# Graph network layers on one core: the rows of stage 2 turned by 32x32 blocks on VectorE, with sixteen SBUF-to-SBUF transfers a group

## The chip, the cores and the metric

The kernel runs on one core of a Trainium2 chip. The metric is the time of one execution on the device in microseconds (us), lower is better. The kernel before takes 2451.24 us, the median of three runs (2449.91 to 2452.41).

## What is computed

`x` holds 50000 nodes of 256 channels in float32, `edge_attr` 12500 edges, sorted by `dst`. Cut to what matters:

```
h   = relu(layernorm(x))                       # rows
agg = scatter-add over dst of relu(h[src] + edge_attr)
z   = (h + agg) @ W1 + b1                      # 50000 x 512
r   = relu(batchnorm(z))                       # statistics over all nodes
y   = r @ W2 + b2                              # 50000 x 256
x1  = x + h + relu(graph norms of y)           # statistics over all of y
h1  = relu(layernorm(x1))
out = x1 + relu(h1 @ W + segment_sum((h1 @ M)[src], dst))
```

## The kernel before, in words

Nodes are worked on in 98 groups of 512 (four rows to each of 128 partitions; the last group is smaller). Stage 1 (to about 435 us) makes the layer norm factors and the batch statistics and writes the edge sums to a table in HBM. Stage 2 (about 440 to 1600 us) is where the change is. Stage 3 makes `x1` and `h1 @ W`, stage 4 does the edges of the second layer.

Each engine has its own program, and they meet through counting semaphores. For a group k of stage 2:

- SyncE (SP) issues, in this order in one step: the load of the rows x of group k (line 975), which from group 12 on waits until the write of the same buffer, four groups earlier, has landed (line 974); the write of x + h of group k-3 (line 982), which waits for GpSimd's addition; the write of y of group k-6 (line 989); and a blank write (line 993). Groups 0 to 7 stay in SBUF and are not written.
- GpSimd (POOL) waits until the rows of group k-2 have been turned (line 1011), clears `ar`, gathers the edge sums of group k into it with four indirect transfers (line 1020), and then adds h to x for group k-2 (line 1032).
- ScalarE (ACT) makes h from x (`norm`, line 1052), two groups ahead.
- VectorE (DVE) adds h and the gathered sums into `ar` (`add`, line 1132), two groups ahead.
- TensorE (PE) turns `ar` with eight 128x128 transposes into PSUM (`turn`, line 1252), one group ahead. ACT copies this into `tH` in the rounded format fp32r (`keep_high`, line 1094), and DVE takes the rest of it into `tL` (`keep_low`, line 1143).
- TensorE does 24 matmuls with W1 in four quarters m (`hidden`, line 1268), each quarter followed by six matmuls of the group before with W2 (`output`, line 1284). ACT drains each quarter of `hidden` (line 1067), DVE splits it into a high part (`high`, line 1175) and a low part (`low`, line 1184), ACT drains y (line 1081), and DVE takes its statistics (`stats`, line 1155).

The order on DVE in one step k is: statistics 0 of group k-2, `keep_low` of k+1, statistics 1, `high` and `low` 0 and 1 of k, `add` of k+2, `high` and `low` 2 and 3. On ACT it is: y of k-2, `keep_high` of k+1, then `hidden` 0, two pieces of `norm` of k+2, `hidden` 1, two pieces, `hidden` 2 and 3. `ar` and `tH` and `tL` have two buffers each; `r32` and the PSUM targets of a quarter have one.

`rounds` writes the first rounds of four groups out and runs the rest in a loop on the engine; the number written out is `NPEEL` (one round for TensorE).

Of the kernel before, what the change touches and what calls it, by code (L numbers as in the profile page):

```python
# [12 lines left out]
P = 128  # L13
# [16 lines left out]
CA = CH + 16  # L30

# [112 lines left out]
def gnn_kernel(nc, x, src, dst, edge_attr, W1, b1, bn_gamma, bn_beta, W2, b2, ln_w, ln_b,  # L144
# [13 lines left out]
    with ExitStack() as ctx:  # L158
# [32 lines left out]
        Ws = sb("Ws", [P, KC, CH])  # L191
        Ms = sb("Ms", [P, KC, CH])
# [33 lines left out]
        loaded = sem("loaded")  # L226
# [72 lines left out]
        with ExitStack() as scope, nc.Block() as block:  # L299
# [130 lines left out]
            def _(pool):  # L430
# [78 lines left out]
                pool.wait_ge(loaded, 16 * 2)  # L509
# [5 lines left out]
            def _(act):  # L515
# [75 lines left out]
                act.dma_start(Ws[:], W.rearrange("(k p) n -> p k n", p=P)).then_inc(loaded, 16)  # L591
                act.dma_start(Ms[:], M.rearrange("(k p) n -> p k n", p=P)).then_inc(loaded, 16)
# [298 lines left out]
        def turn_over(pe, target, times):  # L891

            for _ in range(times):
                pe.matmul(target, ident[:], Ws[:].rearrange("p a b -> p (a b)"), start=True, stop=True)  # L894
# [16 lines left out]
        NPEEL = KEPT // NU + 2  # L911
# [3 lines left out]
        def stays(k):  # L915
            return is_int(k) and k < KEPT

# [9 lines left out]
        h2_done = sem("h2_done")  # L927
        t2_made = sem("t2_made")
# [11 lines left out]
        with ExitStack() as scope, nc.Block() as block:  # L940
# [21 lines left out]

            @block.sync
            def _(sp):

                def step(at):
# [36 lines left out]
            def _(pool):  # L1003

                def step(at):
                    if inside(at, NG):
# [4 lines left out]
                        after(pool, t2_made, k - AU + 1)  # L1011
# [26 lines left out]
            def _(act):  # L1038
# [46 lines left out]
                def keep_high(at):  # L1085
                    if not inside(at, NG):
                        return
                    k = at[0]
                    s, _ = ring(at, 2)
                    n = columns(k)  # L1090
                    act.wait_ge(t2_made, k + 1)
                    after(act, z_made, (k - 1) * HC)
                    for c in range(KC):
                        last = act.activation(tH[:, s, c, 0:n], hT_ps[:, c, 0:n], ACT.Copy)
# [28 lines left out]
            def _(dve):  # L1123
# [11 lines left out]
                def keep_low(at):  # L1135
# [6 lines left out]
                    for c in range(KC):  # L1142
                        last = dve.tensor_tensor(tL[:, s, c, 0:n], hT_ps[:, c, 0:n],
                                                 tH[:, s, c, 0:n].bitcast(FP32), ALU.subtract)
                    last.then_inc(tl_kept, 1)

# [40 lines left out]
                def step(at):  # L1187
                    stats(back(at, 2), 0)
                    keep_low(back(at, -1))
# [5 lines left out]
                    add(back(at, -2))  # L1195
                    high(at, 2)
# [39 lines left out]
                add((1, 1, 0, NU))  # L1236
                keep_low((0, 0, 0, NU))
# [3 lines left out]
            def _(pe):  # L1241
                def turn(at):
                    if not inside(at, NG):
# [5 lines left out]
                    after(pe, tl_kept, k)  # L1249
# [63 lines left out]
                rounds(pe, step, WHOLE - 2, NU, 1, NG - WHOLE + 2 + 1)  # L1313
# [26 lines left out]

        xy_in = [sem(f"xy_in{s}") for s in range(RL)]
# [32 lines left out]
        with ExitStack() as scope, nc.Block() as block:  # L1374
# [24 lines left out]
            def _(sp):  # L1399
# [258 lines left out]
            def _(pe):  # L1658
                def step(at):
# [304 lines left out]
```

## Time and profile before

| | |
|---|---|
| median of 3 runs | 2451.24 us |
| span of the profiled execution | 2446.4 us |
| PE busy | 2354.5 us (96%) |
| DVE busy | 2052.5 us (84%) |
| ACT busy | 1713.3 us (70%) |
| POOL busy | 1708.5 us (70%) |
| SP's queue q1 | 182434 packets, 459.36 MB, 51.2% of 16 DMA engines |

The profile gives one execution's span from its first to its last instruction and no other time of it; the median of the runs stands 4.8 us above that span. Busy time counts an instruction from start to end, with time in which it is held up inside. PE is the matmuls, PEld the weight loads beside them. SPq is the issue of a transfer on SP: its duration is the engine's time for the issue, not that of the transfer. The granted clock of TensorE is 1.00 at 2.4 GHz and would be 0.50 at 1.2 GHz; a stretch that mixes the two stands between.

### The profile page before, as it was taken

How to read it: one execution, taken by the hardware profiler on the slowest of the kernel's cores; microseconds unless marked ns; L12 is line 12 of the kernel's file. 1: busy time of each engine (PE TensorE's matmuls, PEld its weight loads, DVE VectorE, ACT ScalarE, POOL GpSimd, SP SyncE). 2: the span in 40 equal slices, each digit the busy share in tenths (PEclk: the TensorE clock that was granted, in tenths of full speed). 3: DMA queues.
4: the chain of work that ended last, by engine and by line, in shares of the span. 5: the costliest groups of instructions: out<-in, count | busy, mean ns of one | idle time of the engine just before them, and what ended most of it. 6: DMA issues, size and time to landing. Idle time of an engine off the chain costs nothing. (4 is left out here: it accounts for less than half of the span.)

```text
span 2446.4 us, 48745 instructions
## 1 busy us (share of the span) xinstructions
PE 2354.5 (96%) x12271; PEld 2013.5 (82%) x12271; DVE 2052.5 (84%) x5707; ACT 1713.3 (70%) x3449; POOL 1708.5 (70%) x1599
## 2 busy tenths in 40 slices
PE   7999998799999999999999999979999999989997
PEld 6888886588888888888888888858989888969996
DVE  8999997598888888888888888967777777749996
ACT  6999997466666666666666666638888888846664
POOL 5777777577767667767766666717777777767774
PEclk8999999899999999999999999999999999999999
DMA  8888995323444444444444344349999999765662
GB/s 257 283 278 275 278 277 170 124 58 127 152 150 158 163 151 147 146 146 166 153 147 145 145 164 154 141 173 405 405 411 413 413 413 413 294 197 162 173 177 88
DMA packets 242978, 531.73 MB, mean 217 GB/s; under 512 B 53856, under 2 KB 141177, under 8 KB 231442
## 3 DMA queue, kind: packets, MB, share of 16 engines
q1 hardware_dynamic: 182434, 459.36, 51.2%
q0 software_dynamic: 59808, 70.24, 10.2%
q8 instruction: 50, 0.82, 0.1%
q14 instruction: 94, 0.77, 0.1%
q10 hardware_dynamic: 592, 0.54, 0.1%
HBM read 340.23 MB, written 286.84 MB: 256 GB/s over the span
## 5 line engine op out<-in xcount | busy, mean ns | idle before, releaser
L1020 POOL DMA_INDIRECT ar<-sum_table,idx x392 | 462.3, 1179 | 177.6 <-issue 96.5
L1067 ACT ACTIVATE r<-pair,bnC,bnA 128x512 f32<-128x512 f32 x392 | 305.9, 781 | 380.2 <-PE pair L1268 377.7
L1471 POOL DMA_INDIRECT x1d_table<-x1r,slot x392 | 383.8, 979 | 139.8 <-issue 123.9
L1175 DVE CAST rH<-r 128x512 fp32r<-128x512 f32 x392 | 391.0, 997 | 97.7 <-ACT r L1067 97.7
L1694 PE MATMUL pair<-Ws,h1T 128*128 128x256 f32 x1568 | 358.7, 382 | 8.9 <-DVE orr L1602 7.4
L1694 PEld LDWEIGHTS pair<-Ws,h1T 128*128 128x128 f32 x1568 | 290.2, 190 | 52.1 <-issue 14.3
L1284 PE MATMUL bank<-rH,W2h 128*128 128x512 f32 (+1 forms) x784 | 305.6, 390 | 1.8 <-ACT yr L1081 1.8
L1284 PE MATMUL bank<-rL,W2h 128*128 128x512 f32 (+1 forms) x784 | 305.7, 390 | 0.0
L1284 PE MATMUL bank<-rH,W2l 128*128 128x512 f32 (+1 forms) x784 | 305.0, 389 | 0.0
L836 PE MATMUL bank<-hr 128*128 128x257 f32 (+1 forms) x1568 | 274.2, 329 | 9.6 <-ACT hr L535 9.6
L1184 DVE TENSOR_TENSOR rL<-r,rH 128x512 fp32r<-128x512 f32 x392 | 271.1, 691 | 13.5
L836 PEld LDWEIGHTS bank<-hr 128*128 128x128 f32 x1568 | 251.3, 192 | 36.6 <-ACT hr L535 10.3
L1268 PE MATMUL pair<-tH,W1h 128*128 128x512 f32 (+1 forms) x784 | 250.7, 401 | 0.0
L1268 PE MATMUL pair<-tH,W1l 128*128 128x512 f32 (+1 forms) x784 | 242.7, 391 | 0.0
L1268 PE MATMUL pair<-tL,W1h 128*128 128x512 f32 (+1 forms) x784 | 241.3, 389 | 0.0
L1602 DVE SCALAR_TENSOR_TENSOR orr<-pair,x1r 128x1024 f32<-128x1024 f32 x98 | 120.0, 1224 | 138.2 <-DMA out<-orr 79.5
L1032 POOL TENSOR_TENSOR xr<-xr,hr 128x1024 f32<-128x1024 f32 x90 | 219.9, 2444 | 7.1 <-ACT hr L1052 4.9
L1013 POOL MEMSET ar<- 128x1024 f32 x98 | 95.3, 973 | 173.0 <-PE pair L1252 158.5
L1529 ACT ACTIVATE h1r<-x1r,n,r 128x256 f32<-128x256 f32 x392 | 202.6, 593 | 0.0
L535 ACT ACTIVATE hr<-xr,nmr,rstd 128x256 f32<-128x256 f32 x392 | 202.3, 586 | 0.2
L1052 ACT ACTIVATE hr<-xr,nmr,rstd 128x256 f32<-128x256 f32 x360 | 195.7, 596 | 0.0
L1284 PEld LDWEIGHTS bank<-rH,W2h 128*128 128x128 f32 x784 | 147.3, 188 | 32.6 <-ACT yr L1081 2.5
(239 smaller groups left out, 5234.1 us busy)
## 6 DMA issues: line engine op xcount, KB each, us to landing
xr<-in_x SPq DMA_DIRECT2D x186, 512.0 KB, 3.9
xy_kept<-xy_table SPq DMA_DIRECT2D x57, 1024.0 KB, 20.7
x_table<-x1r SPq DMA_DIRECT2D x97, 512.0 KB, 19.8
out<-orr SPq DMA_DIRECT2D x97, 512.0 KB
xy_table<-xr SPq DMA_DIRECT2D x89, 512.0 KB, 2.6
xy_table<-yr SPq DMA_DIRECT2D x89, 512.0 KB, 3.3
xyr<-xy_table SPq DMA_DIRECT2D x32, 1024.0 KB, 21.0
sum_table<-e_tot SPq DMA_DIRECT2D x99, 128.0 KB, 4.5
```

The source lines that it names most:

```text
L535: last = act.activation(hr[0:p, h, j, 0:CH], xr[0:p, s, j, :], ACT.Relu, bias=nmr[0:p, bass.ds(k * T + j, 1)], scale=rstd[0:p, bass.ds(k * ...
L836: return pe.matmul(o, a, b, start=False, stop=False, skip_group_check=True)
L1020: pool.indirect_dma_start(ar[0:p, s, j, :], None, sum_table[:, :], bass.IndirectOffsetOnAxis(ap=idx[0:p, s, j:j + 1], axis=0), bounds_chec ...
L1032: pool.tensor_tensor(xbuf(k, s)[0:p, 0:n, :], xbuf(k, s)[0:p, 0:n, :], hr[0:p, h, 0:n, :], ALU.add).then_inc(xh2_done, 1)
L1067: act.activation(r32[:, m, 0:n], z_ps[m][:, 0:n], ACT.Relu, bias=bnC[:, m:m + 1], scale=bnA[:, m:m + 1]).then_inc(r_kept, 1)
L1175: dve.tensor_copy(rH[:, s, m, 0:n], r32[:, m, 0:n]).then_inc(rh_kept, 1)
L1184: dve.tensor_tensor(rL[:, s, m, 0:n], r32[:, m, 0:n], rH[:, s, m, 0:n].bitcast(FP32), ALU.subtract).then_inc(rl_kept, 1)
L1268: last = pe.matmul(z_ps[m][:, 0:n], w[:, c, m * P:(m + 1) * P], t[:, s, c, 0:n], start=i == 0, stop=i == len(parts) - 1)
L1284: last = pe.matmul(y_ps[c][:, 0:n], w[:, m, c * P:(c + 1) * P], t[:, s, m, 0:n], start=m == 0 and i == 0, stop=m == HC - 1 and i == 2)
L1471: pool.indirect_dma_start(x1d_table[:, :], bass.IndirectOffsetOnAxis(ap=slot[0:p, part, s * T + j:s * T + j + 1], axis=0), x1r[0:p, s, j, ...
L1529: last = act.activation(h1r[0:p, f, j, :], x1r[0:p, s, j, :], ACT.Relu, bias=n3[0:p, s, j:j + 1], scale=r3[0:p, s, j:j + 1])
L1694: last = pe.matmul(tile_of(pair[2], j)[0:p, :], h1T[:, s, c, j * p:j * p + p], Ws[:, c, :], start=c == 0, stop=c == KC - 1)
```

## The change

TensorE's transposes stay for the first and the last group only. For groups 1 to 96, VectorE turns `ar` in blocks of 32x32 in one instruction (`turn_blocks`) into one buffer `blocks` (the place of W2s). Then SP exchanges the quarters of partitions with sixteen transfers (`move_blocks`), each from 32 partitions to 32 partitions in two pieces of 512 B, 32 KB in all, into one of two buffers `staged` (the places of the stage 3 weights and of W1s). ACT and DVE read `tH` and `tL` from there and not from PSUM. `keep_high` moves behind quarter 1 on ACT, `keep_low` behind `add` on DVE, with `turn_blocks` of the next group behind it. GpSimd's wait for the turned rows becomes one for `blocks_made`. Stage 2 is written out in full on every engine. The weights W and M of stage 3 are loaded at the start of that stage.

```diff
-        NPEEL = KEPT // NU + 2
+        NPEEL = NG
+        def by_tensor(k):
+            return is_int(k) and k in (0, NG - 1)
+        blocks = W2s[:].rearrange("p a b -> p (a b)")
+        staged = [WM[:].rearrange("p a b c -> p (a b c)"), W1s[:].rearrange("p a b -> p (a b)")]
...
+            def turned_part(k, s, c, n):
+                if by_tensor(k):
+                    return hT_ps[:, c, 0:n]
+                return staged[s][:, c * GC:(c + 1) * GC].rearrange("p (q t n) -> p t q n", q=QUADS, t=T)
...
+                def move_blocks(at):
+                    if not inside(at, NG) or by_tensor(at[0]):
+                        return
+                    k = at[0]
+                    s, _ = ring(at, 2)
+                    sp.wait_ge(blocks_made, k)
+                    if is_int(k) and k == 1:
+                        sp.wait_ge(q_made, 1)
+                    after(sp, tl_kept, k - 1)
+                    for q in range(QUADS):
+                        for b in range(QUADS):
+                            here = blocks[q * SQ:(q + 1) * SQ, :].rearrange("p (c b n) -> p c b n", c=KC, b=QUADS)
+                            there = staged[s][b * SQ:(b + 1) * SQ, :].rearrange("p (c q n) -> p c q n", c=KC, q=QUADS)
+                            sp.dma_start(there[:, :, q, :], here[:, :, b, :]).then_inc(ht_in[s], 16)
...
                     three = back(at, 3)
+                    move_blocks(three)
                     if inside(three, NG) and not stays(three[0]):
...
-                        after(pool, t2_made, k - AU + 1)
+                        if is_int(k) and k == AU:
+                            pool.wait_ge(t2_made, 1)
+                        else:
+                            after(pool, blocks_made, k - AU)
...
-                    act.wait_ge(t2_made, k + 1)
+                    if by_tensor(k):
+                        act.wait_ge(t2_made, 1 if k == 0 else 2)
+                    else:
+                        act.wait_ge(ht_in[s], 16 * QUADS * QUADS * turned_before(at))
...
                     keep_y(back(at, 2))
-                    keep_high(back(at, -1))
                     pieces = norm(back(at, -2))
                     for m in range(HC):
                         hidden(at, m)
                         for piece in (pieces[0:2], pieces[2:4], [], [])[m]:
                             piece()
+                        if m == 1:
+                            keep_high(back(at, -1))
...
+                def turn_blocks(at):
+                    if not inside(at, NG) or by_tensor(at[0]):
+                        return
+                    k = at[0]
+                    s, _ = ring(at, AU)
+                    other, _ = ring(back(at, 1), 2)
+                    dve.wait_ge(h2_done, k + 1)
+                    after(dve, ht_in[other], 16 * QUADS * QUADS * turned_before(back(at, 1)))
+                    dve.transpose(blocks.rearrange("p (b t n) -> p t b n", b=KC * QUADS, t=T),
+                                  ar[:, s, :, :].rearrange("p t (b n) -> p t b n", n=SQ)).then_inc(blocks_made, 1)
...
                     stats(back(at, 2), 0)
-                    keep_low(back(at, -1))
                     stats(back(at, 2), 1)
                     high(at, 0)
                     low(at, 0)
                     high(at, 1)
                     low(at, 1)
                     add(back(at, -2))
+                    keep_low(back(at, -1))
+                    turn_blocks(back(at, -2))
                     high(at, 2)
...
-                    if not inside(at, NG):
+                    if not inside(at, NG) or not by_tensor(at[0]):
                         return
...
-                rounds(pe, step, WHOLE - 2, NU, 1, NG - WHOLE + 2 + 1)
+                rounds(pe, step, WHOLE - 2, NU, NPEEL, NG - WHOLE + 2 + 1)
...
+                sp.dma_start(Ws, W.rearrange("(k p) n -> p k n", p=P)).then_inc(w_loaded, 16)
+                sp.dma_start(Ms, M.rearrange("(k p) n -> p k n", p=P)).then_inc(w_loaded, 16)
...
+                        if is_int(k) and k == 0:
+                            pe.wait_ge(w_loaded, 32)
```

## Rows read from the trace of the kernel before

**Rows 1.** Windows: stretch, busy us (instructions) of each engine, clock, DMA share, GB/s.

```profile
1000.00:1200.00 200.00, 200.00 (x952) 167.04 (x951) 172.69 (x221) 122.99 (x204) 138.70 (x119) 1.00 0.43 151
...
2100.00:2200.00 100.00, 89.17 (x484) 74.56 (x483) 60.47 (x201) 63.22 (x131) 69.84 (x73) 0.97 0.62 218
```

**Rows 2.** Timeline of PE in stage 2: start, length, line, work, count.

```profile
475.10 0.40 PE L1284 MATMUL bank<-rH,W2h 128*128 128x512 f32 x1
...
484.65 1.03 PE L1252 MATMUL pair<-ident,ar 128*128 128x128 f32 x8
485.44 0.71 PE L1268 MATMUL pair<-tH,W1h 128*128 128x512 f32 x2
```

**Rows 3.** Groups of instructions, 700 to 1500 us (68 groups of nodes).

```profile
L1020 POOL DMA_INDIRECT ar<-sum_table,idx x272 | 316.4, 1163 | 125.0 <-issue 68.0 <-POOL idx L1014 56.9
L1175 DVE CAST rH<-r 128x512 fp32r<-128x512 f32 x271 | 267.5, 987 | 64.3 <-ACT r L1067 64.3
...
L1184 DVE TENSOR_TENSOR rL<-r,rH 128x512 fp32r<-128x512 f32 x271 | 187.8, 693 | 9.3
...
L1032 POOL TENSOR_TENSOR xr<-xr,hr 128x1024 f32<-128x1024 f32 x68 | 166.7, 2451 | 1.6
...
L1143 DVE TENSOR_TENSOR tL<-pair,tH 128x512 fp32r<-128x512 f32 x136 | 87.3, 683 | 6.4 <-ACT tH L1094 5.4
...
L1132 DVE TENSOR_TENSOR ar<-ar,hr 128x1024 f32<-128x1024 f32 x68 | 83.4, 1227 | 0.0
...
L1013 POOL MEMSET ar<- 128x1024 f32 x68 | 66.5, 977 | 116.9 <-PE pair L1252 116.7
...
L1014 POOL COPY idx<-ids 128x4 int32 x68 | 12.2, 179 | 0.0
```

**Rows 4.** Waits of SP's queue, 700 to 1500 us: total, times, longest.

```profile
SPq L982 <- POOL xr L1032: 565.6, 67, 10.7
SPq L975 <- DMA xy_table<-xr: 62.9, 68, 1.1
```

**Rows 5.** Timeline of SP's issues, about one step of stage 2.

```profile
1111.20 0.33 SPq L982 DMA_DIRECT2D xy_table<-xr  x1
...
1113.95 0.35 SPq L975 DMA_DIRECT2D xr<-in_x  x1
```

**Rows 6.** Timeline of POOL, ACT and DVE in the same step.

```profile
1108.10 3.21 DVE L1175 CAST rH<-r 128x512 fp32r<-128x512 f32 x1 [0.39 <-ACT r L1067]
1108.61 2.40 POOL L1032 TENSOR_TENSOR xr<-xr,hr 128x1024 f32<-128x1024 f32 x1
...
1111.95 0.42 DVE L1175 CAST rH<-r 128x512 fp32r<-128x512 f32 x1
...
1112.46 1.09 ACT L1094 ACTIVATE tH<-pair 128x512 fp32r<-128x512 f32 x2
...
1113.62 1.27 DVE L1143 TENSOR_TENSOR tL<-pair,tH 128x512 fp32r<-128x512 f32 x2
```

**Rows 7.** Timelines of issues without a wait between them: stage 1, then stage 2.

```profile
1.87 0.41 SPq L391 DMA_DIRECT2D src_rows<-in_src  x1
...
3.92 0.36 SPq L395 DMA_DIRECT2D id_table<-no_rows  x1
...
33.77 0.27 ACTq L589 DMA_DIRECT2D vec_rows<-in_L_gnn_bn_gamma  x1
...
36.28 0.41 ACTq L591 DMA_DIRECT2D Ws<-in_L_gnn_W  x1
...
447.80 0.46 SPq L993 DMA_DIRECT2D x1d_table<-blank  x1
448.30 0.43 SPq L975 DMA_DIRECT2D xy_kept<-in_x  x1
```

**Rows 8.** Transfers: what, queue, count, KB each, median us to landing.

```profile
xy_table<-xr SPq DMA_DIRECT2D x89, 512.0 KB, 2.6
...
id_table<-no_rows SPq DMA_DIRECT2D x1, 196.0 KB, 2.1
```

More of the change, by code:

```diff
@@ L30 @@
 CA = CH + 16
+SQ = 32
+QUADS = P // SQ
 def back(at, lag):
@@ L190, in gnn_kernel @@
         W2l = sb("W2l", [P, HC, CH], FP32R, scope=weights, side="right")
-        Ws = sb("Ws", [P, KC, CH])
-        Ms = sb("Ms", [P, KC, CH])
+        WM = sb("WM", [P, 2, KC, CH])
+        Ws, Ms = WM[:, 0, :, :], WM[:, 1, :, :]
         vec = sb("vec", [P, 24])
@@ L893, in turn_over @@
             for _ in range(times):
-                pe.matmul(target, ident[:], Ws[:].rearrange("p a b -> p (a b)"), start=True, stop=True)
+                pe.matmul(target, ident[:], W1s[:, 0, :], start=True, stop=True)
         next_phase()
@@ L916, in stays, with turned_before @@
             return is_int(k) and k < KEPT
+        def by_tensor(k):
+            return is_int(k) and k in (0, NG - 1)
+        def turned_before(at):
+            s, used = ring(at, 2)
+            return used + s
+        blocks = W2s[:].rearrange("p a b -> p (a b)")
+        staged = [WM[:].rearrange("p a b c -> p (a b c)"), W1s[:].rearrange("p a b -> p (a b)")]
         x2_in = [sem(f"x2_in{s}") for s in range(NU)]
@@ L927, in gnn_kernel @@
         h2_done = sem("h2_done")
+        blocks_made = sem("blocks_made")
+        ht_in = [sem(f"ht_in{s}") for s in range(2)]
         t2_made = sem("t2_made")
@@ L961, in ybuf, with nodes_of @@
                 return y_part(xy_kept[:, k, :, :]) if stays(k) else yr[:, s, :, :]
+            def turned_part(k, s, c, n):
+                if by_tensor(k):
+                    return hT_ps[:, c, 0:n]
+                return staged[s][:, c * GC:(c + 1) * GC].rearrange("p (q t n) -> p t q n", q=QUADS, t=T)
+            def nodes_of(part, k):
+                return part if by_tensor(k) else part.rearrange("p (t q n) -> p t q n", q=QUADS, t=T)
             @block.sync
             def _(sp):
+                def move_blocks(at):
[12 more added lines that the diff above has]
+                            sp.dma_start(there[:, :, q, :], here[:, :, b, :]).then_inc(ht_in[s], 16)
                 def step(at):
@@ L1090, in keep_high @@
                     n = columns(k)
-                    act.wait_ge(t2_made, k + 1)
+                    if by_tensor(k):
+                        act.wait_ge(t2_made, 1 if k == 0 else 2)
+                    else:
+                        act.wait_ge(ht_in[s], 16 * QUADS * QUADS * turned_before(at))
                     after(act, z_made, (k - 1) * HC)
                     for c in range(KC):
-                        last = act.activation(tH[:, s, c, 0:n], hT_ps[:, c, 0:n], ACT.Copy)
+                        last = act.activation(nodes_of(tH[:, s, c, 0:n], k), turned_part(k, s, c, n), ACT.Copy)
                     last.then_inc(th_kept, 1)
@@ L1142, in keep_low @@
                     for c in range(KC):
-                        last = dve.tensor_tensor(tL[:, s, c, 0:n], hT_ps[:, c, 0:n],
-                                                 tH[:, s, c, 0:n].bitcast(FP32), ALU.subtract)
+                        last = dve.tensor_tensor(nodes_of(tL[:, s, c, 0:n], k), turned_part(k, s, c, n),
+                                                 nodes_of(tH[:, s, c, 0:n].bitcast(FP32), k), ALU.subtract)
                     last.then_inc(tl_kept, 1)
+                def turn_blocks(at):
[8 more added lines that the diff above has]
+                                  ar[:, s, :, :].rearrange("p t (b n) -> p t b n", n=SQ)).then_inc(blocks_made, 1)
                 def stats(at, c):
@@ L1236, in _ @@
                 add((1, 1, 0, NU))
+                turn_blocks((1, 1, 0, NU))
                 keep_low((0, 0, 0, NU))
```

6 lines of the change are left out of this document (1 added, 5 removed).

## Prediction

> **What bounds the kernel now.** I read the windows first, to find which engine fills stage 2. In 1000 to 1200 us PE is busy all the time, at a granted clock of 1.00, DVE 172.7 us of 200, and the DMA engines 0.43 of it [rows 1]. 952 matmuls and transposes at 56 a group are 17 groups, so one group takes 200/17 = 11.76 us. The reader is to see that no other engine is near 100%: stage 2 goes at PE's pace. The timeline of PE then tells what the transposes cost. From 475.10 to 484.65 there are 42 matmuls, so one takes 9.55/42 = 0.227 us, and the 48 of a group 10.9 us [rows 2]. What is left of 11.76, about 0.87, is the eight transposes (the next matmul starts 0.79 us after the first of them). That is what the change can win: 0.87 x 96 = 84 us, if PE stays the bound.
>
> The groups of instructions and the timelines give the other engines' work in a group. On DVE, all starts to ends sum to 172.7/17 = 10.2 us. One cast in four takes 3.2 us and not 0.42, the one that meets GpSimd's addition [rows 6], so some 1.9 us of the 10.2 (the mean of 0.99 less 0.42 and four casts, less overlaps) is being held up, and 8.3 is work. The waits of SP's queue say that SP has idled 565.6/67 = 8.4 us a group before line 982, for GpSimd's addition, and 0.9 us before line 975, for a landing [rows 4]. So there is room on SP, but it stands inside a fixed order.
>
> **What goes.** The transposes go from PE, 0.87 us a group. So does ACT's and DVE's reading of PSUM for `tH` and `tL`; I cost these unchanged, at 1.09 and 1.27 us a group [rows 6], since the subtract with both operands in SBUF takes 693 ns against 683 [rows 3]. The loops on the engines go too; they were hidden behind PE, and the code written out adds only fetches, so I take nothing. W and M move to the start of stage 3, where PE needs them only at the seventh step and 512 KB are little beside the group loads; stage 1 loses the same transfer. Nothing again.
>
> **What comes.** On DVE, one turn of 128x1024 in blocks. No row shows it. The nearest is the addition of the same shape, 1.23 us; the cheapest row by element is the cast, 0.42 for 512 or 0.84, and the dearest sensible bound is two passes, 2.5. I take 1.25. DVE then has 10.2 + 1.25 = 11.45 us a group with all its hold-ups, 9.5 without.
>
> The Trainium skill ("VectorE: DVE Perf Modes", The three transpose paths) gives 311 ns for one 128x128 on VectorE in two-byte data and notes that it does only separate 32x32 blocks. Eight of them would be an estimate of 2.5 us; one instruction instead of eight should save most of the fixed part. No run here shows either, and the price of it is among the rivals.
>
> On SP, sixteen issues a group. Seven without a wait from 1.87 to 3.92 started 0.34 apart on average (six steps), eight on ACT from 33.77 to 36.28 0.31 apart, and in stage 2 one starts 0.50 after the one before it [rows 7]. The new ones have 32 partitions in two pieces, between the small and the large ones: 0.37 each, bounds 0.31 and 0.50. Landing after the start of the last issue: 2.1 us for the small table and 2.6 for 512 KB [rows 8]; I take 2.0, as no HBM is in it, bounds 1.5 and 2.6. The sixteen are then through 15 x 0.37 + 2.0 = 7.55 us after the first. Bytes are no issue: 64 pieces of 512 B to each of 16 DMA engines, at a share of 0.43 so far.
>
> **The new ring.** This decides. `turn_blocks` of group k+1 stands behind `keep_low` of k on DVE. That waits for `keep_high` of k on ACT, this waits for the landing of the sixteen of k, and these wait for `turn_blocks` of k. There is only one buffer `blocks` and one group in flight, so one period is at least: SP woken 0.19 (line 1032 ends at 1108.61 + 2.40 = 1111.01 [rows 6], line 982 starts at 1111.20 [rows 5]), transfers 7.55, ACT 1.09 and about 0.1 of waking, DVE's `keep_low` 1.27 and 0.05, turn 1.25. Sum 11.5 us. PE would run at that, 0.26 faster than now and not 0.87. What is queued behind: on ACT `hidden` 2 and 3, on DVE `high` and `low` 2 and 3. They have most of a period before PE wants them, since `output` of a group comes one step later.
>
> **A second ring through SP's order.** `move_blocks` of k stands on SP behind the load at line 975, which waits until the write at line 982 of group k-1, issued in the step before, has landed; and that write waits for GpSimd's addition of k-1. GpSimd can start that step only when `turn_blocks` of k-1 is done. From there: waking 0.1, clearing 0.98, copy 0.18, four gathers 4 x 1.163, the idle before them 125.0/68 = 1.84, addition 2.45, in all 10.2 [rows 3]; SP woken 0.2; from line 982 to line 975 2.75 [rows 5]; issue of 975 and a gap 0.4. So the moves of k can't start before 13.55 us after the turn of k-1. In the old kernel this order cost nothing, since SP had nothing urgent after line 975.
>
> Let the moves start d after their turn. The first ring gives P = 11.5 + d, the second d = 13.55 - P. So P = (11.5 + 13.55)/2 = 12.53 us, and d = 1.03. The write of x+h starts with group 8, so this holds for about 88 groups: 88 x (12.53 - 11.76) = +67 us. Groups 1 to 8 go by the first ring alone: 8 x (11.5 - 11.76) = -2. The first moves land before the gather of group 2, which set the second step before, so 0 at the start. The sum is +65 on a span of 2446.4, thus 2511; the runs' median is 4.8 above the span, so 2516 us.
>
> PE then stands still 1.6 us in each 12.5. In 2100 to 2200 us it is busy 89% and its clock still 0.97 [rows 1], so I take no loss from the clock.
>
> **The rivals.**
>
> A, the forecast: two rings, 2516 us. For: all pieces but the turn and the landing have rows of their own kind. Chance 0.48.
>
> B, the issue is dear: issues of this kind start 0.6 apart, and land 2.0 later. First ring 0.19 + 11.0 + 1.19 + 1.32 + 1.25 = 14.95, over 13.55, so d = 0 and P = 14.95: +3.19 x 96 = +306, 2757 us. For it: lines 982 to 975 of the loop are never as close as 0.37. Against: these lines have waits, and those without are at 0.31 to 0.50. Already at 0.50 the first ring is 13.45 and P 13.5, 88 x 1.74 + 8 x 1.69 = +167, 2618 us. Chance 0.12 for more than that.
>
> C, the turn takes 2.5 us. First ring 12.75, P = 13.15, 88 x 1.39 + 8 x 0.99 = +130, 2581 us. Against: all elementwise rows of DVE in float32 are at 1.2 us for 1024. Chance 0.14.
>
> D, it ends faster: the transfers are through early enough. If issues are 0.28 apart and the last lands after 1.5, the first ring is 9.65 and P by both rings is 11.6: 96 x (11.6 - 11.76) = -15, 2436 us. With shorter ones still, DVE is the bound with its 11.45, and 96 x (11.45 - 11.76) = -30 gives 2421 us, the price I take. It decides from a first ring under 9.97, since (9.97 + 13.55)/2 is 11.76. For: SP is idle most of the period, and DVE's hold-ups may fall when its casts miss the addition. Against: 5 us for sixteen issues is already the low row. Chance 0.17.
>
> The Trainium skill ("DMA: Bandwidth & Descriptors", Issuing engines are not separate DMA queues) says that the time to initiate a DMA is usually small relative to the DMA itself. By that rule the sixteen issues would nearly vanish and D would be the forecast. The trace does not bear it out for transfers of 32 KB: their data are 4 pieces of 512 B on each DMA engine, and an issue is 0.3 us or more [rows 7].
>
> E, PE stays the bound: 10.9 a group, -0.87 x 96 = -84, 2367 us. DVE's hold-ups of 1.9 us would have to vanish, and both rings too. Chance 0.05. A draw within 0.2% (5 us, about what a measurement of this kernel tells from no change) has 0.04.
>
> **Range and chances.** 2516 is A's. The range 2418 to 2625 takes A, C, the draw and most of D, and leaves B and E out; A's own range, with issues from 0.34 to 0.41, is 2493 to 2548. Slower: A, B, C, 0.74; same 0.04; faster 0.22.
>
> **What would show it.** The period in stage 2 (L1184 on DVE, four a group): 12.5 us. SP: sixteen issues 0.37 apart in one block, and lines 982 and 975 just ahead of it, with the landing wait before 975 now on the path. ACT's line of `keep_high` waits for a DMA, DVE's `keep_low` for ACT, and PE's first `hidden` for DVE, some 1.6 us a group. Casts of 3.2 us become rarer. I am wrong if the moves start right at the end of the turn (the second ring isn't there, P 11.5, 2426 us), if the issues are not 0.31 to 0.50 apart, if the turn is not 0.84 to 2.5 us, or if PE's granted clock in stage 2 falls.

## The result, and the profile after

The changed kernel takes 2805.15 us (median of four runs, 2802.59 to 2808.51) against 2451.23: a ratio of 1.1444 (1.1428 to 1.146), 354 us slower. The sign was forecast; the size, +65 us, was not, and the time lies far outside the range of 2418 to 2625. The profiled execution has a span of 2806.8 us.

A window of stage 2 of the kernel after, with the columns of [rows 1]:

```profile
1000.00:1200.00 200.00, 161.43 (x618) 127.61 (x618) 132.65 (x183) 93.09 (x156) 103.92 (x92) 0.90 0.46 151
```

Stage 2 now has 48 matmuls a group, so 618 are 12.875 groups, and one takes 200/12.875 = 15.53 us where it took 11.76. (15.53 - 11.76) x 96 = 362 us, against 354 measured: the loss is all in stage 2. No engine fills it: PE has fallen from 200 busy to 161, DVE from 173 to 133 [rows 1]. A period that no engine fills is a ring of waits. The waits of the kernel after from 900 to 1700 us show its members (engine, what it works on, line, what it waited for: us in total, times, longest):

```profile
POOL ar L1054 <- DVE W2s L1201: 286.4, 51, 6.7
DVE tL L1188 <- ACT tH L1138: 186.8, 51, 7.1
...
PE pair L1326 <- DVE tL L1188: 157.0, 51, 5.2
ACT tH L1138 <- DMA W1s<-W2s: 143.1, 26, 7.6
ACT tH L1138 <- DMA WM<-W2s: 143.0, 26, 7.4
```

PE waits for `keep_low` (L1188), this for `keep_high` (L1138), and this, 5.5 us a group, for the transfers out of `blocks` (the place of W2s). The timeline of SP in the kernel after shows what these wait for:

```profile
1205.26 0.33 SPq L1012 DMA_DIRECT2D xr<-in_x  x1
...
1207.27 10.21 SPq L1001 DMA_DIRECT2D W1s<-W2s  x16
...
1220.42 0.33 SPq L1012 DMA_DIRECT2D xr<-in_x  x1
...
1222.45 11.07 SPq L1001 DMA_DIRECT2D WM<-W2s  x16
```

Sixteen issues take 10.21 us, 0.64 each, and not 0.37. SP reaches them early: its load (L1012) is out at 1205.26 and it then waits for the turn. The block after it takes 11.07 us, since one issue in it is long:

```profile
1223.73 1.47 SPq L1001 DMA_DIRECT2D WM<-W2s  x1
```

The trace shows what the long ones go with. From 461 to 1945 us, the stretch of the 96 blocks, the view of the DMA queues has this line for the loads of code (packets, MB, share of 16 engines):

```profile
q8 instruction: 37, 0.61, 0.2%
```

Each of these 37 loads of 16 KB falls into a different block of issues. The 37 blocks with one take 11.02 us on average, the 59 others 10.24; in the two blocks above, the second has such a load and the first has none. The kernel before has 6 such loads in its stage 2 (440 to 1600 us), so most of them come from the code written out. They add some 37 x 0.78 = 29 us to the ring, an estimate from these means. The run with filler matmuls below bears it out.

The same period on DVE, ACT and PE of the kernel after:

```profile
1206.01 1.24 DVE L1201 STREAM_TRANSPOSE W2s<-ar 128x1024 f32<-128x1024 f32 x1
...
1218.80 1.15 ACT L1138 ACTIVATE tH<-W1s 128x512 fp32r<-128x512 f32 x2 [6.42 <-DMA W1s<-W2s]
...
1219.98 1.29 DVE L1188 TENSOR_TENSOR tL<-W1s,tH 128x512 fp32r<-128x512 f32 x2 [5.86 <-ACT tH L1138]
...
1221.19 1.24 DVE L1201 STREAM_TRANSPOSE W2s<-ar 128x1024 f32<-128x1024 f32 x1
...
1221.33 1.22 PE L1326 MATMUL pair<-tH,W1h 128*128 128x512 f32 x2 [4.01 <-DVE tL L1188]
```

This is the whole ring. The turn ends at 1207.25, and the first issue starts at 1207.27 (0.02). `keep_high` starts 11.53 later, which is 1.9 after the start of the last issue. `keep_low` follows after 1.18, the next turn after 1.21, and that ends after 1.24: 0.02 + 11.53 + 1.18 + 1.21 + 1.24 = 15.18 us, 15.5 with the longer blocks. The two matmuls after the wait of 4.0 us take 1.22 us where two took 0.71 [rows 2]; the granted clock of the stretch is 0.90, a mixture of the levels of 2.4 and 1.2 GHz.

The groups of instructions of the kernel after, from 900 to 1700 us, beside [rows 3]:

```profile
L1232 DVE CAST rH<-r 128x512 fp32r<-128x512 f32 x205 | 114.1, 557 | 55.5 <-ACT r L1108 55.5
L1177 DVE TENSOR_TENSOR ar<-ar,hr 128x1024 f32<-128x1024 f32 x52 | 113.6, 2184 | 0.0
```

GpSimd's addition now often meets `add` (2.18 us on average, 1.23 before) and seldom a cast (0.56, 0.99 before).

### The profile page after: what moved, and what is told of

Its sections match the earlier page's. It is cut to its first block and busy times, and to the rows that moved or that the text cites. A ratio compares the mean times of both kernels' runs of the same rounds, so it can differ in the third digit from the quotient of the medians.

```text
span 2806.8 us, 46351 instructions
## 1 busy us (share of the span) xinstructions
PE 2417.9 (86%) x11503; PEld 2009.8 (72%) x11503; DVE 2074.2 (74%) x5803; ACT 1702.4 (61%) x3449; POOL 1693.2 (60%) x1599
## 5 line engine op out<-in xcount | busy, mean ns | idle before, releaser
L1326 PE MATMUL pair<-tH,W1h 128*128 128x512 f32 (+1 forms) x784 | 279.1, 440 | 303.9 <-DVE tL L1188 303.9
L1061 POOL DMA_INDIRECT ar<-sum_table,idx x392 | 422.7, 1078 | 177.9 <-issue 98.2
L1326 PEld LDWEIGHTS pair<-tH,W1h 128*128 128x128 f32 x784 | 155.4, 210 | 371.7 <-DVE tL L1188 340.4
L1757 PE MATMUL pair<-WM,h1T 128*128 128x256 f32 x1568 | 359.8, 382 | 7.5 <-DVE orr L1663 5.6
L1757 PEld LDWEIGHTS pair<-WM,h1T 128*128 128x128 f32 x1568 | 289.4, 189 | 54.5 <-issue 16.1
L1232 DVE CAST rH<-r 128x512 fp32r<-128x512 f32 x392 | 221.4, 565 | 110.5 <-ACT r L1108 110.5
L1326 PE MATMUL pair<-tL,W1h 128*128 128x512 f32 (+1 forms) x784 | 266.0, 423 | 0.0
L1138 ACT ACTIVATE tH<-WM 128x512 fp32r<-128x512 f32 x96 | 55.1, 621 | 264.9 <-DMA WM<-W2s 264.9
L1138 ACT ACTIVATE tH<-W1s 128x512 fp32r<-128x512 f32 x96 | 55.1, 621 | 262.0 <-DMA W1s<-W2s 262.0
L535 ACT ACTIVATE hr<-xr,nmr,rstd 128x256 f32<-128x256 f32 x392 | 202.4, 587 | 0.4 <-PE bank L834 0.4
```

The costliest lines, as they stand in the source:

```text
L535: last = act.activation(hr[0:p, h, j, 0:CH], xr[0:p, s, j, :], ACT.Relu, bias=nmr[0:p, bass.ds(k * T + j, 1)], scale=rstd[0:p, bass.ds(k * ...
L1061: pool.indirect_dma_start(ar[0:p, s, j, :], None, sum_table[:, :], bass.IndirectOffsetOnAxis(ap=idx[0:p, s, j:j + 1], axis=0), bounds_chec ...
L1232: dve.tensor_copy(rH[:, s, m, 0:n], r32[:, m, 0:n]).then_inc(rh_kept, 1)
L1326: last = pe.matmul(z_ps[m][:, 0:n], w[:, c, m * P:(m + 1) * P], t[:, s, c, 0:n], start=i == 0, stop=i == len(parts) - 1)
L1757: last = pe.matmul(tile_of(pair[2], j)[0:p, :], h1T[:, s, c, j * p:j * p + p], Ws[:, c, :], start=c == 0, stop=c == KC - 1)
```

## The experiments

Theories at the start: the ring through the sixteen issues, whose price depends on the transfer's form (T1); the clock of TensorE, lowered by the waits (T2); the code written out (T3); SP's order (T4). Where a period is given, it comes from the count of matmuls in windows of 200 us, as above.

**The price of an issue by itself.** A block between stages 1 and 2 of the kernel before issues batches of transfers on SP with no wait between them:

```diff
+                def batch(pairs):
+                    for there, here in pairs:
+                        sp.dma_start(there, here).then_inc(priced, 16)
+                        count[0] += 16
+                    sp.wait_ge(priced, count[0])
```

> The kernel before with a small stage of its own ahead of stage 2, in which SyncE issues batches of transfers back to back and waits after each batch: 16 x (32 partitions, 2 pieces of 512 B, SBUF to SBUF, the shape of the change), 16 x (32 partitions, 1 piece of 1 KB), 16 x (32 partitions, 4 pieces of 256 B), 16 x (32 partitions, 2 pieces, HBM to SBUF), 16 x the same SBUF to HBM, 4 x (128 partitions, 2 pieces), 4 x (128 partitions, 1 piece), 16 x (8 partitions, 4 KB), 8 x (16 partitions, 4 KB). Theory (the issue on SyncE is dear by the shape of the transfer): the change's shape is 0.64 us apart here too, with nothing else on the DMA engines; one piece of 1 KB is cheaper, some 0.45, and four pieces dearer, 0.9 or more. Rival (the queue pushes back because the DMA engines are busy in stage 2): alone, the change's shape is issued 0.35 to 0.40 apart. The whole kernel is 50 to 90 us longer than before.

Timeline of SP in that kernel (`one_b` and `two_b` are in SBUF, `shelf` in HBM):

```profile
444.51 10.40 SPq L915 DMA_DIRECT2D two_b<-one_b  x16
...
456.19 10.07 SPq L915 DMA_DIRECT2D two_b<-one_b  x16
...
467.53 10.30 SPq L915 DMA_DIRECT2D two_b<-one_b  x16
...
479.12 10.11 SPq L915 DMA_DIRECT2D two_b<-shelf  x16
...
502.53 2.70 SPq L915 DMA_DIRECT2D two_b<-one_b  x4
```

The first batch is the change's own exchange, here with nothing else running: 10.40 us. So neither contention nor SP's place in the kernel makes it dear. One piece of 1 KB (the second) or four of 256 B (the third) cost the same, and so does HBM as the source with two pieces of 512 B (the fourth). Four transfers of 128 partitions cost 0.67 each, about as much as those of 32. The issues of [rows 7] are cheaper, so a second list looked at transfers with HBM at one end and one piece a partition.

> The kernel before with another small stage of batches on SyncE ahead of stage 2, to find which property of a transfer makes its issue 0.60 and not 0.43: 4 x (128 partitions of 1 KB) to one contiguous run of HBM, to rows 4 KB apart, and the same two from HBM to SBUF; 8 x (32 partitions of 1 KB) and 4 x back; 8 x (8 partitions of 1 KB); 8 x (one partition) to HBM, from HBM and from SBUF to SBUF; 4 x (32 partitions) SBUF to SBUF. Theory (an issue is cheap where the HBM side is one contiguous run, and dear where both sides are cut into rows): contiguous ones 0.43 to 0.48 apart at any number of partitions, all the others 0.60 to 0.65. Rival (any batch of issues through one semaphore with nothing between is 0.6 apart): all of them 0.60 to 0.65.

The same view of the second kernel: HBM to SBUF from 128 partitions, SBUF to HBM from 32, 8 and 1, then SBUF to SBUF of one partition and of 32, two of each:

```profile
454.67 0.43 SPq L915 DMA_DIRECT2D two_b<-shelf  x1
455.15 0.43 SPq L915 DMA_DIRECT2D two_b<-shelf  x1
...
463.61 0.42 SPq L915 DMA_DIRECT2D shelf<-one_b  x1
464.08 0.42 SPq L915 DMA_DIRECT2D shelf<-one_b  x1
...
470.62 0.30 SPq L915 DMA_DIRECT2D shelf<-one_b  x1
470.95 0.29 SPq L915 DMA_DIRECT2D shelf<-one_b  x1
...
474.09 0.25 SPq L915 DMA_DIRECT2D shelf<-one_b  x1
474.39 0.25 SPq L915 DMA_DIRECT2D shelf<-one_b  x1
...
482.84 0.59 SPq L915 DMA_DIRECT2D two_b<-one_b  x1
483.47 0.59 SPq L915 DMA_DIRECT2D two_b<-one_b  x1
...
486.36 0.59 SPq L915 DMA_DIRECT2D two_b<-one_b  x1
486.99 0.59 SPq L915 DMA_DIRECT2D two_b<-one_b  x1
```

From start to start: 0.48 (128 partitions), 0.47 (32), 0.33 (8) and 0.30 (1) with HBM at one end and one piece a partition, and 0.63 with SBUF at both ends, even for one partition and 1 KB. The expectation that a contiguous side in HBM makes it cheap fell: strided and contiguous batches of 128 partitions were both 0.47.

**Fewer issues.** Four transfers of 128 partitions carry the same bytes. This kernel leaves out the exchange of quarters between partitions, so its result is another one.

```diff
-                    for q in range(QUADS):
-                        for b in range(QUADS):
...
+                    for b in range(QUADS):
+                        here = blocks.rearrange("p (c b n) -> p c b n", c=KC, b=QUADS)
+                        there = staged[s].rearrange("p (c q n) -> p c q n", c=KC, q=QUADS)
+                        sp.dma_start(there[:, :, b, :], here[:, :, b, :]).then_inc(ht_in[s], 16)
```

> The changed kernel with the same bytes and the same pieces of 512 B moved by four transfers of 128 partitions instead of sixteen of 32; the quarters are then not exchanged, so its result is another one. Theory (a fixed price for each issue): four issues of about 0.7 us; the first ring falls from 15.2 to about 7.7 us, and the period to what VectorE or TensorE sets, 10.9 to 11.5: 2370 to 2430 us. Rival (the price follows the pieces or the bytes): the four take as long as the sixteen, the period stays at 15 to 15.5, 2780 to 2810 us.

2518.51 us, 1.0271 (1.0254 to 1.0288), period 12.5. Twelve issues fewer take 287 of the 354 us away. Timeline of that kernel, SP, DVE and POOL:

```profile
1203.52 3.28 SPq L1000 DMA_DIRECT2D WM<-W2s  x4
...
1210.54 2.42 POOL L1072 TENSOR_TENSOR xr<-xr,hr 128x1024 f32<-128x1024 f32 x1
1210.59 3.52 DVE L1187 TENSOR_TENSOR tL<-WM,tH 128x512 fp32r<-128x512 f32 x2 [0.94 <-ACT tH L1137]
...
1214.04 1.23 DVE L1200 STREAM_TRANSPOSE W2s<-ar 128x1024 f32<-128x1024 f32 x1
...
1215.62 0.33 SPq L1011 DMA_DIRECT2D xr<-in_x  x1
1216.06 2.66 SPq L1000 DMA_DIRECT2D W1s<-W2s  x4
```

Here both rings of the forecast are seen. The turn ends at 1215.27, but the moves start at 1216.06, behind the load at L1011, which has waited for a landing: the second ring. Before them the turn of the group before ended at 1202.77, so this ring is 1216.06 - 1202.77 = 13.29 (forecast 13.55). The first, from the start of the moves at 1203.52 to the end of the turn, is 11.75, and (11.75 + 13.29)/2 = 12.52, as measured. (The two add up to two periods by construction; what they show is which waits make each.) There is a new price in the first: `keep_low` takes 3.52 us and not 1.29, with GpSimd's addition starting beside it.

**One issue.** The same with a single transfer, again without the exchange:

```diff
-                        sp.dma_start(there[:, :, b, :], here[:, :, b, :]).then_inc(ht_in[s], 16)
+                    sp.dma_start(staged[s], blocks).then_inc(ht_in[s], 16)
```

> The changed kernel with the same 512 KB moved by one transfer of 128 partitions of 4 KB instead of sixteen; the quarters are not exchanged, so its result is another one. Theory (beyond the issues, the late place of keep_low costs something of its own, since GpSimd's addition then holds up VectorE on the way to TensorE's next group): not the 10.9 us of TensorE alone, but near the 12.5 of four transfers: 12.0 to 12.6, 2475 to 2530 us. Rival (all of the change's cost is the issues): 10.9 to 11.5, 2370 to 2430 us.

2511.98 us, 1.0249 (1.0233 to 1.0265). Three issues less give next to nothing more, so what is left of the change with one issue, 61 us, is something else. Timeline of that kernel:

```profile
1217.70 3.64 DVE L1184 TENSOR_TENSOR tL<-W1s,tH 128x512 fp32r<-128x512 f32 x2 [0.81 <-ACT tH L1134]
1217.77 2.41 POOL L1069 TENSOR_TENSOR xr<-xr,hr 128x1024 f32<-128x1024 f32 x1
```

`keep_low` reads both operands from SBUF now and stops for all of the addition. From PSUM it took 1.27 [rows 6], where it did not meet the addition; a run below, the kernel before with the addition moved, lets them meet, and it takes 1.29. This agrees with the Trainium skill ("SBUF — State Buffer", SBUF: two separate sides), which says that a VectorE operation with two SBUF inputs and a GpSimd operation that reads SBUF take the shared ports as an exclusive lock for the whole instruction.

**One piece instead of two.** `blocks` and `staged` laid out so that each transfer has one piece of 1 KB; the turn in two instructions.

```diff
-                            sp.dma_start(there[:, :, q, :], here[:, :, b, :]).then_inc(ht_in[s], 16)
+                            sp.dma_start(there[:, q, :], here[:, b, :]).then_inc(ht_in[s], 16)
```

> The changed kernel with the two halves of the channels laid side by side, so that each of the sixteen transfers moves 32 partitions in one piece of 1 KB instead of two of 512 B; the turn on VectorE is two instructions of 128x512. Theory (two pieces a partition make the issue dear): issues 0.45 to 0.48 apart, the first ring 2.5 us shorter and 0.1 longer by the second turn, 12.8; with the second ring at 13.9 the period is about 13.3, 2600 us. Rival (the count of transfers alone): issues stay 0.64 apart and the time within 20 us of 2815.

2790.98 us, 1.1383 (1.1364 to 1.1402); two blocks of sixteen issues next to each other take 10.14 and 10.41 us. My idea that the second piece made them dear fell here.

**The turn out of the ring.** On DVE, `turn_blocks` ahead of `keep_low`:

```diff
+                    turn_blocks(back(at, -2))
                     keep_low(back(at, -1))
-                    turn_blocks(back(at, -2))
```

> The changed kernel with turn_blocks of group k+1 ahead of keep_low of group k on VectorE, nothing else. Theory (the period is the ring through the single buffer: turn, sixteen issues, landing, keep_high, keep_low, turn): keep_high and keep_low, 1.15 and 1.3 us, leave the ring, which falls to 0.05 + 9.6 + 1.95 + 1.25 = 12.85 us; SyncE's own step (10.2 for the moves, 3.3 for the rest with the landing it waits for) is then the bound with 13.5: 96 x (13.5 - 11.76) over before, 2618 us. Rival (TensorE's lowered clock or VectorE sets the pace): no change beyond 20 us from 2805.

2653.37 us, 1.0823 (1.0805 to 1.0841), period 13.9. The turn still waits until the transfers have emptied `blocks`, so the ring is now issues, landing and turn. With the write of x + h a step later and the load behind the moves besides:

```diff
+                    four = back(at, 4)
...
+                    move_blocks(three)
...
-                    three = back(at, 3)
-                    move_blocks(three)
```

> The changed kernel with two things moved: turn_blocks ahead of keep_low on VectorE, and on SyncE the write of x+h one step later and ahead of the moves, the load of x behind them. No work is left out. Theory (turn first leaves SyncE's step and its wait for a landing as the bound): the ring of turn, issues and landing is 12.85, SyncE's step without the landing wait 10.25 + 0.6 + 0.45 + 0.72 + 0.43 = 12.45, so the period is 12.9: 2451 + 96 x 1.14 = 2560 us. Rival (VectorE's hold-ups by GpSimd's addition set the pace): the period stays at the 13.9 of turn first alone, 2650 us.

2650.67 us, 1.0819 (1.0801 to 1.0837): nothing more, so SP's order (T4) costs nothing while sixteen issues are in the ring. Timeline of this kernel:

```profile
1207.28 1.25 DVE L1202 STREAM_TRANSPOSE W2s<-ar 128x1024 f32<-128x1024 f32 x1
...
1208.56 11.28 SPq L1001 DMA_DIRECT2D W1s<-W2s  x16
...
1221.22 1.25 DVE L1202 STREAM_TRANSPOSE W2s<-ar 128x1024 f32<-128x1024 f32 x1 [1.03 <-DMA W1s<-W2s]
```

0.03 + 11.28 + 1.38 to the next turn + 1.25 = 13.94: the ring has lost `keep_high` and `keep_low`. The expectation put it at 12.85, with 9.6 to the start of the last issue; in this kernel that is 10.5 on average.

**The clock and the code.** Fourteen filler matmuls in each step of PE, whose result is overwritten, keep it busy (T2); and the kernel before with stage 2 written out (T3):

```diff
+                    if 2 <= at[0] < NG - 4:
+                        for _ in range(14):
+                            pe.matmul(hT_ps[:, 0, :], W1h[:, 0, 0:P], W1h[:, 0, :], start=True, stop=True)
```

> The changed kernel with 14 matmuls more on TensorE at the start of each step 2 to 93, into a PSUM bank that nobody reads, while it would wait for keep_low. Theory (TensorE is not in the ring, its lowered clock costs nothing): the granted clock in stage 2 rises from 0.90 to 0.98 or more and the time stays within 20 us of 2805. Rival (the lowered clock after each wait costs part of the period): with the clock up the time falls by 30 to 60 us.

```diff
-        NPEEL = KEPT // NU + 2
+        NPEEL = NG
...
-                rounds(pe, step, WHOLE - 2, NU, 1, NG - WHOLE + 2 + 1)
+                rounds(pe, step, WHOLE - 2, NU, NPEEL, NG - WHOLE + 2 + 1)
```

> The kernel before with stage 2 written out in full on every engine instead of in loops, nothing else. Theory: the loops cost nothing and the code written out costs nothing, 2451 us within 5. Rival (fetching the code of stage 2 slows the engines): 2465 us or more.

The first has a granted clock of 0.99 in 1200 to 1400 us, where the kernel after has 0.91, and takes 2814.11, 1.1484 (1.1465 to 1.1503): with the clock up nothing is won, since PE waits anyway. T2 fell. The second takes 2451.36, 0.9998 (0.9989 to 1.0008): code written out costs nothing in the kernel before, where SP has time to spare.

For the changed kernel this does not settle T3. The fillers are code of PE alone, and they raised the loads of code (here from 461 to 1955 us):

```profile
q8 instruction: 47, 0.77, 0.2%
```

Ten loads more, and each again falls into a block of its own: the 47 blocks with one take 11.07 us on average, the 49 others 10.22. All blocks together take 1021 us and not 1012, and the kernel is 9 us slower. So a load of PE's code stretches the issue that SP has under way, and T3 has about 30 of the 354 us. No run keeps the change and loops PE's code, which would show this alone.

**The exchange through HBM.** Four writes of 32 partitions into a buffer in HBM and one load back, with the turn first and the load late as well. Nothing is left out of the computation here.

```diff
-                        for b in range(QUADS):
...
+                        here = blocks[q * SQ:(q + 1) * SQ, :].rearrange("p (c b n) -> p c b n", c=KC, b=QUADS)
+                        there = halfway[s].rearrange("(b p) (c q n) -> q p c b n", b=QUADS, c=KC, q=QUADS)[q]
+                        sp.dma_start(there, here).then_inc(hb_out, 16)
...
+                    sp.wait_ge(hb_out, 16 * QUADS * at[0])
+                    sp.dma_start(staged[s], halfway[s]).then_inc(ht_in[s], 16)
```

> As turn first and load late, and the quarters are exchanged through HBM: four writes (32 partitions, eight pieces of 512 B) that put each group into its turned order in a table, and one load of 128 partitions of 4 KB. Five issues instead of sixteen. No work is left out. Theory (the sixteen issues are the cost of the change, not the turn on VectorE): writes and landing 4.3, load and landing 2.8, so no ring is over 10 us, and VectorE (9.6 us of work and about 2 held up by GpSimd) sets 11.5: 2425 us. Rival (VectorE is over its limit with the turn): 12 or more, 2475 us or above.

2561.14 us, 1.045 (1.0433 to 1.0467), period 12.9. DVE and POOL in its timeline:

```profile
1207.39 3.27 DVE L1242 CAST rH<-r 128x512 fp32r<-128x512 f32 x1 [0.96 <-ACT r L1118]
1207.97 2.40 POOL L1083 TENSOR_TENSOR xr<-xr,hr 128x1024 f32<-128x1024 f32 x1
```

SP is out of the ring. It now runs over DVE and PE: `keep_low`, PE's `hidden` 0 and 1, the cast of quarter 1, held up to 3.27 us by the addition, `low` 1, `add`, the turn, and `keep_low` again. I tried to shorten this ring in four ways. First, `keep_high` behind `hidden` 0 and `keep_low` ahead of `add` and the turn:

```diff
-                        if m == 1:
+                        if m == 0:
                             keep_high(back(at, -1))
...
+                    keep_low(back(at, -1))
                     high(at, 1)
```

> As the exchange through HBM, with keep_high behind hidden 0 on ScalarE and keep_low behind low 0 on VectorE, so that TensorE gets the next group earlier. Theory (the ring runs through the late keep_low): the ring is cut, and VectorE's own step of 9.6 us of work and 2 to 2.8 held up is the bound: 11.5 to 12.4, middle 12.0, 2475 us. Rival (only the hold-up matters, not the place): 12.9, 2561 us.

2807.5 us, 1.1443 (1.1424 to 1.1462): with `keep_low` ahead of the turn the landing is in the ring again, here with a write and a load in a row (8.15 us of waiting on ACT at `keep_high`). The turn ahead of `keep_low` is worth more than an earlier `keep_low`. The addition in four pieces, alone and with this order:

```diff
+                        for j in range(n):
+                            last = pool.tensor_tensor(xbuf(k, s)[0:p, j, :], xbuf(k, s)[0:p, j, :],
+                                                      hr[0:p, h, j, :], ALU.add)
```

> As the exchange through HBM, with GpSimd's addition of h to x (128x1024, 2.4 us) issued as four additions of 128x256. Theory (the 12.9 us that the exchange through HBM still took are a ring on VectorE and TensorE: keep_low, hidden 0 and 1, the cast of quarter 1, which GpSimd's addition holds up for 2.85 us, low 1, add, turn, keep_low): a shorter addition frees the cast after at most one piece, the ring falls to 10.8 and the period to 10.9 to 11.3, 2370 to 2410 us. Rival (GpSimd keeps VectorE out over all four pieces, or the ring is not this one): 12.9 us a group, 2550 to 2570 us.

> Both edits to the exchange through HBM: GpSimd's addition in four and keep_low early. Theory: no ring over 10.9, VectorE 9.6 us of work and under 1 held up, so TensorE's 10.9 us without its transposes is the bound: 10.9 to 11.2, 2365 to 2400 us, faster than the kernel before. Rival (the landing of the load comes too late for the earlier keep_high): 11.8 or more, 2455 us or above.

Alone it gives 2460.22 us, 1.0029 (1.0019 to 1.004), period 11.7: most of the hold-up is gone (this cast takes 0.93 us), but the four pieces take 4.49 us, and POOL waits for the turn only 5.4 us of the 600 from 900 to 1500. With the other order it is 2807.58, 1.1444 (1.1425 to 1.1463). In two halves:

> As the exchange through HBM with GpSimd's addition in two of 128x512 instead of four of 128x256. Theory (with four, GpSimd itself became the bound, its four additions taking 4.5 us instead of 2.4 since each meets VectorE; with two they take about 3.0, and VectorE is held up 1.2 us at most): GpSimd's step falls from 11.56 to about 10.3, the ring on VectorE is about 11.2: 2400 to 2430 us, faster than the kernel before. Rival (VectorE's hold-up comes back as GpSimd's falls): 11.7 or more, 2450 us or above.

2575.47 us, 1.0505 (1.049 to 1.0519). Timeline, DVE and POOL:

```profile
1200.64 3.42 DVE L1246 CAST rH<-r 128x512 fp32r<-128x512 f32 x1 [0.96 <-ACT r L1122]
1201.22 2.54 POOL L1086 TENSOR_TENSOR xr<-xr,hr 128x512 f32<-128x512 f32 x2
```

The cast is kept out over both halves. Last, the whole addition ahead of the gathers, so that it meets another instruction, and this edit alone in the kernel before and in the changed one:

```diff
+                        addition(at)
...
-                    two = back(at, 2)
-                    if inside(two, NG):
```

> As the exchange through HBM, with GpSimd's addition of h to x moved from behind the four gathers to ahead of them, so that it meets other work of VectorE (high and low 2 and 3 and the statistics, for which TensorE does not wait yet) and not the cast of quarter 1. No work is left out. Theory (the 2.85 us that this cast is held up stand in the ring keep_low, hidden 0 and 1, high 1, low 1, add, turn, keep_low, and are the rest of the change's cost): the ring falls to 10.1 and the period to VectorE's own sum, 9.6 of work, up to 2 held up and some waits, 11.5 to 12.0: 2430 to 2475 us. Rival (a hold-up of VectorE costs the same wherever it stands): 12.9, 2550 to 2570 us.

> The kernel before with GpSimd's addition ahead of the gathers, nothing else. Theory (before, TensorE sets 11.76 us and VectorE's hold-ups are hidden): 2451 us within 5, so the gain of the last version comes from the turn on VectorE and not from this order. Rival (the order alone is the gain): 2430 us or less.

> The changed kernel with GpSimd's addition ahead of the gathers, nothing else. Theory (with sixteen issues the ring through SyncE sets the period and the place of the addition does not matter): 2805 us within 15. Rival (the hold-up of VectorE is part of the change's cost with sixteen issues too): 2750 us or less.

2417.05 us, 0.9864 (0.9848 to 0.9881): 1.4% faster than the kernel before. The two others are 2450.57, 1.0002 (0.9993 to 1.0011), and 2804.66, 1.1453 (1.1436 to 1.1471): moving the addition gives nothing in either, and 144 us with the ring open (2561.14 to 2417.05). The kernel before with this edit, its window and then POOL and DVE:

```profile
1000.00:1200.00 200.00, 200.00 (x952) 166.89 (x951) 142.29 (x221) 122.97 (x204) 142.57 (x120) 1.00 0.44 152
```

```profile
1116.78 2.41 POOL L1014 TENSOR_TENSOR xr<-xr,hr 128x1024 f32<-128x1024 f32 x1
1117.03 1.29 DVE L1151 TENSOR_TENSOR tL<-pair,tH 128x512 fp32r<-128x512 f32 x2 [0.17 <-ACT tH L1102]
```

DVE is busy 142 us and not 173 [rows 1], so most of its hold-ups are gone, and the time is the same: they cost nothing while PE fills the period. And `keep_low` with one operand in PSUM runs through the addition at 1.29 us. This is the counterpart of the 3.64 above. The fast kernel's window and timeline, POOL and DVE:

```profile
1200.00:1400.00 200.00, 197.39 (x849) 157.48 (x848) 196.48 (x246) 129.74 (x213) 142.83 (x124) 1.00 0.80 250
```

```profile
1203.96 2.57 POOL L1062 TENSOR_TENSOR xr<-xr,hr 128x1024 f32<-128x1024 f32 x1
1204.30 2.78 DVE L1259 TENSOR_TENSOR rL<-r,rH 128x512 fp32r<-128x512 f32 x1
...
1210.31 0.53 DVE L1250 CAST rH<-r 128x512 fp32r<-128x512 f32 x1
```

The addition now holds up a `low` that nobody waits for at once. The period is 11.31. DVE and PE are both busy nearly all the time (196 and 197 of 200 us), but from 900 to 1500 us DVE waits for another engine 2.3 us in all, and PE's weight loads wait 31.6 us for `keep_low`: DVE is the bound.

## Why the prediction was wrong

- **The failed step: sixteen issues at 0.37, bounds 0.31 and 0.50.** Measured 0.64, and 0.69 in a block with a load of code. [rows 7] were read too low twice. Three of the seven issues from 1.87 us move one row of at most 216 B, which pulls their mean down; for 32 partitions with HBM at one end the price is 0.47. And these transfers have SBUF at both ends, which no row had: 0.64. In the prediction's own sum, as an estimate, 0.47 gives a first ring of 13.0, a period of 13.3 and 2594 us, within the range; 0.64 gives a ring and period of 15.55 and 2815 us, near the 2805 measured. Rival B had the mechanism (0.6 apart, ring 14.95, no wait through SP's order, 2757 us), at a chance of 0.12. The ring was 15.18 to 15.5. The four-transfer run shows what twelve issues cost: 287 of 354 us. A term with sixteen copies on the ring needed a wide bound from above: 0.1 us on the price of one is 150 us on the kernel, at 16 x 96. The trace before had rows for one: in stage 3 an issue of `x_table<-x1r` holds SP for 1.2 us in the median and 4.3 at most.
- **The first ring** was right in its members and near in every other term: turn 1.25 (1.24), landing 2.0 (1.9), `keep_high` 1.19 (1.18), `keep_low` 1.32 (1.21), waking of SP 0.19 (0.02).
- **The second ring** did not bind: at a first ring of 15 SP reaches the moves early and waits for the turn. That is the plan's own rule, P = first ring where this is above 13.55, and the four-transfer run shows it at 13.29 and the mean of two rings at 12.5.
- **Missed: `keep_low` with both operands in SBUF.** I costed it unchanged by the row of another subtract [rows 3]. In the change it misses the addition (1.29), but with a short ring it meets it and takes 3.5 to 3.6 us. That the four-transfer run has the 12.5 us forecast for the change is luck: its issues took 2.7 us and not some 6, and the hold-up took that room.
- **Turn at 2.5 us (rival C)** did not happen. It is also what the prediction estimated from the price in the Trainium skill ("VectorE: DVE Perf Modes", The three transpose paths), eight times 311 ns: the trace shows half of that, 1.24 us for 128x1024 in one instruction.
- **Initiation is usually small beside the transfer** (the Trainium skill, "DMA: Bandwidth & Descriptors", Issuing engines are not separate DMA queues): the trace does not agree for transfers of 32 KB; one takes 0.64 us to issue, and ACT reads it 1.9 us after that issue started, and ten of the ring's 15 us are sixteen issues in a row.
- **DVE's sum, 11.45**, as the bound once the rings are gone: 11.31 in the fastest version. **Code written out, 0**: true of the kernel before; in the changed one its loads fall on SP's issues, about 30 us. **Clock, no loss**: it fell to 0.90, which I named as a sign of error, and raising it won nothing, as the run with filler matmuls shows. **W and M, start of stage 2, 0**: not tested alone; stage 2 accounts for 362 us by its period against 354 measured, which leaves no loss elsewhere.
- **PE's gain** of 0.87 us a group (rival E) was real but never the bound; at best DVE lets 0.45 of it through.

Open is what sets the price of an issue: two pieces of 512 B from HBM cost as much as SBUF at both ends, but the issue of `Ws` in [rows 7], with two pieces of 1 KB a partition from HBM on ACT's queue, takes 0.41. Open is also how a load of PE's code stretches an issue of SP. No run spread the sixteen issues over two engines.

## What to carry to other kernels

When work is moved off the bound engine, write down the new ring first: every wait from the new operation back to itself, with the number of groups in flight; here two `staged` buffers left the ring as it was, since `blocks` was one. Price the transfers in a ring by their number, their ends, their pieces and their partitions, and where no row has that form, take the widest bound. Put a row of the old kernel beside each term only if the row has the term's size: a mean over issues of one row says little of issues of 32. A cheap reordering (the turn ahead of `keep_low`, the addition ahead of the gathers) can be worth little or nothing alone and decide the sign once the ring is open.

## What the runs showed of the hardware

- An issue on SP, in a row of them: 0.63 to 0.67 us from SBUF to SBUF for 1 to 128 partitions and for pieces from 256 B to 4 KB; with HBM at one end and one piece, 0.47 for 32 and 128 partitions, 0.33 for 8, 0.30 for 1; with HBM and two pieces of 512 B, 0.64.
- A load of 16 KB of code on queue q8 lengthens the issue that SP has under way. Blocks of sixteen issues with one take 11.02 us against 10.24 (37 loads), and 11.07 against 10.22 with fillers on PE (47 loads).
- GpSimd's addition of 128x1024 with two SBUF inputs (2.4 us) holds a VectorE cast (3.27 for 0.42 to 0.53) or a subtract with both operands in SBUF (3.64 for 1.29) for its whole length. The subtract with an operand in PSUM isn't held: 1.29 us beside the addition. Cut in two halves the addition still held a cast for 3.42 us; cut in four it let VectorE in (0.93), and took 4.49 us itself.
- A VectorE transpose of 32x32 blocks, 128x1024 in float32, takes 1.24 us, as an addition of that shape does.
